# A two-layer conditioned-FFN kernel: first loads on three queues, B behind the mixture, and the end reordered

## The reference

```python
# layer 0
h = gelu(cond @ W0 + b0); h = gelu(h @ W1 + b1)
att = softmax(h @ W2 + b2)                          # 128 x 8
agg_w = einsum('bk,koi->boi', att, weight[..., 0]); agg_b = att @ bias_k
t = einsum('boi,bih->boh', agg_w, x) + agg_b[:, :, None]
gates = softmax of the two best of (t @ Wr.T) over 4 experts
x = x + sum_e gates_e * 16/sqrt(16) * (t @ A_e.T) @ B_e.T
# layer 1
o = grouped_conv1d(x, weight, 9 taps, 4 groups) + cond @ c_weight.T + fside
h = relu(layernorm(o @ gw1.T + gb1) * gamma + beta)
g = h @ gw2.T + gb2                                 # 8 experts, top 2, softmax over the two
counts = how often each expert is first, second, over all 4096 rows
w = gates of the experts whose count is at most the capacity
x = x + o @ weight.T + ((o @ lora_A_e) * w_e) @ lora_B_e / 16
```

## Time and profile before

| | us |
|---|---|
| runs of the kernel before, median of 3 | 305.37 (305.17 to 308.9) |
| the profiled execution's own time | 303.87 |
| its span (first to last recorded event) | 302.1 |
| TensorE busy | 290.3 (96%) |
| VectorE busy | 194.9 (64%) |
| ScalarE busy | 125.2 (41%) |
| GpSimd busy | 95.1 (31%) |

### The profile page before, as it was taken

One profiled execution on the slowest core, in us unless ns is written; L12 is line 12 of the kernel. 1 busy time (PEld: TensorE's weight loads), 2 busy tenths in 40 slices (PEclk: granted clock), 3 DMA queues, 4 the chain that ended last, 5 costly groups with the idle time before them and its releaser, 6 DMA issues.

```text
span 302.1 us, 6171 instructions
## 1 busy us (share of the span) xinstructions
PE 290.3 (96%) x1995; PEld 239.7 (79%) x1995; DVE 194.9 (64%) x503; ACT 125.2 (41%) x263; POOL 95.1 (31%) x124
## 2 busy tenths in 40 slices
PE   7999999999999999999999999999999999798994
PEld 6989967787888788879887978797868777586883
DVE  1445984734488448835793579366957645878785
ACT  3417743436523652356235622562256235111330
POOL 4342425132312331143114311431114116216650
PEclk9999999999999999999999999999999999999998
DMA  5696799992779289918892879386538860004887
GB/s 134 196 335 139 169 257 220 235 217 62 218 214 208 54 220 229 192 35 243 207 201 44 242 205 189 55 233 148 136 71 244 174 142 0 0 2 171 322 334 286
DMA packets 74255, 52.75 MB, mean 175 GB/s; under 512 B 44388, under 2 KB 61204, under 8 KB 74232
## 3 DMA queue, kind: packets, MB, share of 16 engines
q1 hardware_dynamic: 72792, 51.37, 67.3%
q10 hardware_dynamic: 1120, 1.07, 1.2%
q0 software_dynamic: 320, 0.02, 0.4%
HBM read 35.67 MB, written 16.78 MB: 174 GB/s over the span
## 4 chain that ended last, share of the span: by engine, by line
PE 65%; SPq 10%; DVE 10%; DMA 6%; issue 4%; ACT 2%; DVEq 0%; ACTq 0%
PE ps_g L1124 13%; PE ps_d L1124 12%; PE ps_c L1264 8%; PE ps_a L1085 6%; PE ps_t L1280 4%; SPq L352 4%; DMA xg<-x1d 3%; PE ps_a L1074 3%; DMA x1d<-xq 3%; PE ps_d L1305 3%; SPq L355 2%; PE ps_d L1306 2%; PE ps_v L1097 2%; PE ps_d L1491 1%; PE ps_d L1487 1%
## 5 line engine op out<-in xcount | busy, mean ns | idle before, releaser
L508 POOL TENSOR_TENSOR o1l<-o,o1h 128x512 fp32r<-128x512 f32 x30 | 39.3, 1311 | 149.3 <-ACT o L639 149.3
L1124 PE MATMUL ps_d<-wt_hi,o1h 128*128 128x336 f32 (+1 forms) x120 | 41.1, 342 | 0.3 <-DVE y_all L950 0.3
L1124 PE MATMUL ps_d<-wt_hi,o1l 128*128 128x336 f32 (+1 forms) x120 | 38.7, 323 | 0.0
L1124 PE MATMUL ps_d<-wt_lo,o1h 128*128 128x336 f32 (+1 forms) x120 | 38.6, 322 | 0.0
L1124 PE MATMUL ps_g<-wt_hi,o1h 128*128 128x336 f32 x112 | 35.7, 319 | 0.6 <-ACT tmp_all L654 0.4
L944 DVE TENSOR_TENSOR oT<-ps_c,biasT 128x512 f32<-128x512 f32 x32 | 21.9, 685 | 21.7 <-PE ps_c L1264 21.7
L1124 PE MATMUL ps_g<-wt_hi,o1l 128*128 128x336 f32 x112 | 35.5, 317 | 0.0
L1124 PE MATMUL ps_g<-wt_lo,o1h 128*128 128x336 f32 x112 | 35.4, 316 | 0.0
L1264 PE MATMUL ps_c<-xg,cw 96*32 96x512 f32 x256 | 34.1, 604 | 1.0 <-DMA xg<-x1d 1.0
L627 ACT ACTIVATE xq<-y_all 128x512 f32 (+1 forms) x29 | 31.8, 1150 | 7.0 <-DMA x1d<-xq 3.7
L1085 PEld LDWEIGHTS ps_a<-pm,xT 128*128 128x128 f32 x256 | 30.2, 192 | 1.4 <-issue 0.8
(11 more groups left out here) (249 smaller groups left out, 582.1 us busy)
## 6 DMA issues: line engine op xcount, KB each, us to landing
xg<-x1d SPq DMA_DIRECT2D x64, 254.0 KB, 4.8
xg<-x1d SPq DMA_DIRECT2D x32, 256.0 KB, 3.7
x1d<-xq SPq DMA_DIRECT2D x30, 256.0 KB, 3.4
xs<-in_x_dram SPq DMA_DIRECT2D x6, 1024.0 KB, 5.9
out_dram<-xT SPq DMA_DIRECT2D x16, 256.0 KB, 2.1
out_dram<-xg SPq DMA_DIRECT2D x16, 256.0 KB, 2.1
y_all<-in_x_dram ACTq DMA_DIRECT2D x2, 512.0 KB, 5.5
y_all<-in_x_dram SPq DMA_DIRECT2D x1, 1024.0 KB, 5.7
```

Of the source, the lines that this page charges most:

```text
L508: pool.tensor_tensor(lo, o1[t % 2][:, :, :], hi.bitcast(fp32), ALU.subtract).then_inc(s_o1l, 1)
L1124: last = T.matmul(bank[:, 0:columns], a[:, Q - 1 - q, :], w[:, q, first:first + columns], start=(q == 0 and n == 0), stop=(q == Q - 1 and ...
```

## The change

1. **First loads.** W2 is issued first on ScalarE's queue; b2 and the second half of x of step 0 go to SyncE's queue, behind W1; the context weights move behind the mixing bias; the four loads of B and the one of fside are issued by GpSimd, ahead of its copy of the mixing weights. SyncE's queue issues 13 loads ahead of the main weights' group where it issued 16, ScalarE's 4 where it issued 6.
2. **TensorE and VectorE at the start.** Three of the dummy product pairs between the attention's products go. The two small context products move from between the attention's products to behind x's transposes; B's transposes and their split move behind the mixture and its bias products.
3. **lora_B.** The high part is made in step 6 on ScalarE, before its last gate copy, the low part on GpSimd behind step 6's last split, into `gms` (now of type fp32r, with bitcasts where it was read as fp32) instead of `o1l`.
4. **Norm, counts, y.** In the last step `norm_last` runs between the one-hot comparison and the count sums of step 6. The counts come from one product over the four one-hot tiles at once (64 columns), and VectorE sums the five groups. y of tiles 1 and 2 is added before the counts are read, y of tile 3 after `lt_lo`.
5. **Last tile.** Its lora products, sum and store are done in two halves of 256 columns, the second in another PSUM bank (`ps_t`).

```diff
@@ SyncE, ScalarE, GpSimd: loads
-            sp.dma_start(ctxn, ctxw).then_inc(s_ld["ctx"], 16)
-            sp.dma_start(w2n, w2).then_inc(s_ld["w2"], 16)
+            sp.dma_start(b2b, b2.partition_broadcast(P)).then_inc(s_ld["b2"], 16)
+            sp.dma_start(xs_early[0][:, NT // 2:NT, :], x_v[0][:, NT // 2:NT, :]).then_inc(s_xh, 16)
...
-            for e in range(E0):
-                sp.dma_start(bn[:, :, e * R0:(e + 1) * R0],
-                             ffb[e].rearrange("(p c) r -> p c r", c=HC)).then_inc(s_ld["bn"], 16)
+            sp.dma_start(ctxn, ctxw).then_inc(s_ld["ctx"], 16)
...
+            for e in range(E0):
+                pool.dma_start(bn[:, :, e * R0:(e + 1) * R0],
+                               ffb[e].rearrange("(p c) r -> p c r", c=HC)).then_inc(s_ld["bn"], 16)
+            pool.dma_start(fsb, fside.partition_broadcast(P)).then_inc(s_ld["side"], 16)
             pool.wait_ge(s_ld["mixw"], 64)
...
+            act.dma_start(w2n, w2).then_inc(s_ld["w2"], 16)
...
-            act.dma_start(b2b, b2.partition_broadcast(P)).then_inc(s_ld["b2"], 16)
             act.dma_start(xs_early[0][:, 0:NT // 2, :], x_v[0][:, 0:NT // 2, :]).then_inc(s_xf, 16)
-            act.dma_start(fsb, fside.partition_broadcast(P)).then_inc(s_ld["side"], 16)
-            act.dma_start(xs_early[0][:, NT // 2:NT, :], x_v[0][:, NT // 2:NT, :]).then_inc(s_xh, 16)
@@ GpSimd and ScalarE: lora_B
-        lb_hi, lb_lo = b_hi, o1l[0][:, :, :].rearrange("p q m -> p (q m)")
+        lb_hi, lb_lo = b_hi, gms[:, :, :, :].rearrange("p t a c -> p (t a c)")
...
                 if at_step(s, NS - 1):
                     rstd(s)
+                if at_step(s, NS - 2):
                     pool.wait_ge(s_lbh, 1)
-                    pool.wait_ge(s_mp, s * NT + 1)
+                    pool.wait_ge(s_gtp, NS)
                     pool.tensor_tensor(lb_lo, lbn, lb_hi[:, :].bitcast(fp32), ALU.subtract).then_inc(s_lb, 1)
...
                 o_hi(s + 1, 0)
+                if at_step(s, NS - 2):
+                    act.wait_ge(s_ld["lora"], 16)
+                    nc.scalar.activation(lb_hi[:, :], lbn, ACT.Copy).then_inc(s_lbh, 1)
                 ga_out(3)
@@ VectorE: norm, counts, y
                     y_out(s, 0)
-                    choices_counted(s - 1)
-                    norm_last(s)
+                    choices_counted(s - 1, lambda: norm_last(s))
                     choices_weighted(s - 1)
...
+            y_out(NS - 1, 1)
+            y_out(NS - 1, 2)
             link, n = chain(dve, s_c3, 0)
             dve.wait_ge(s_cntp, 1)
-            link(V.tensor_scalar(allowed[:, :, :], ps_g[:, 0:2 * E1].rearrange("p (c e) -> p c e", c=2),
-                                 float(CAPACITY), None, ALU.is_le))
+            link(V.reduce_sum(cnt1[:, :, :], ps_g[:, 0:2 * E1 * (NT + 1)]
+                              .rearrange("p (t c e) -> p c e t", c=2, e=E1), AXX))
+            link(V.tensor_scalar(allowed[:, :, :], cnt1[:, :, :], float(CAPACITY), None, ALU.is_le))
...
-            y_out(NS - 1, 1)
-            y_out(NS - 1, 2)
-            y_out(NS - 1, 3)
             dve.wait_ge(s_lth, 1)
             V.tensor_tensor(lt_lo[0][:, :], ps_a[0][:, :], lt_hi[0][:, :].bitcast(fp32), ALU.subtract)\
              .then_inc(s_ltf, 1)
+            y_out(NS - 1, 3)
@@ TensorE: counts, last tile
             pe.wait_ge(s_cnt, 1)
-            for t in range(NT):
-                last = T.matmul(ps_g[:, 0:2 * E1], ones[:, :], oh[:, t, :, :].rearrange("p c e -> p (c e)"),
-                                start=False, stop=(t == NT - 1))
-            last.then_inc(s_cntp, 1)
+            T.matmul(ps_g[:, 0:2 * E1 * NT], ones[:, :], oh[:, :, :, :].rearrange("p t c e -> p (t c e)"),
+                     start=True, stop=True).then_inc(s_cntp, 1)
...
+                if at_step(s, NS - 1):
+                    for cols, bank in ((slice(0, H // 2), ps_l[NT - 1]), (slice(H // 2, H), ps_t)):
+                        high(NT - 1, cols, bank)
+                        low(NT - 1, cols, bank)
```

More of the change, by code:

```diff
@@ L422, in store @@
                 for t in range(NT):
-                    sp.wait_ge(s_yo[t], s + 1)
-                    sp.dma_start(out_v[bass.ds(s * NT + t, 1)].rearrange("n p h -> p (n h)"), yo[par][t])\
-                      .then_inc(s_out[par][t], 16)
+                    parts = 2 if at_step(s, NS - 1) and t == NT - 1 else 1
+                    n = H // parts
+                    for i in range(parts):
+                        sp.wait_ge(s_yo[t], s + i + 1)
+                        sp.dma_start(out_v[bass.ds(s * NT + t, 1)].rearrange("n p h -> p (n h)")[:, i * n:i * n + n],
+                                     yo[par][t][:, i * n:i * n + n]).then_inc(s_out[par][t], 16)
             steps(sp, store, 0, NS - 1)
@@ L903, in choices_counted @@
                     link(chosen)
+                    if between is not None:
+                        between()
                     link(V.reduce_sum(cnt1[:, :, :], oh[:, :, :, :].rearrange("p t c e -> p c e t"), AXX))
@@ L1059, in finish @@
                     for t in range(NT):
[L1060 removed]
                         wait(dve, s_out[par][t], k * 16)
[L1062 to L1063 removed]
+                        parts = 2 if at_step(s, NS - 1) and t == NT - 1 else 1
+                        n = H // parts
+                        for i in range(parts):
+                            dve.wait_ge(s_lp, s * NT + t + i + 1)
+                            V.tensor_tensor(yo[par][t][:, i * n:i * n + n], (ps_l[t], ps_t)[i][:, i * n:i * n + n],
+                                            y_all[:, bass.ds(s * ST + t * H + i * n, n)],
+                                            ALU.add).then_inc(s_yo[t], 1)
             steps(dve, finish, 0, NS - 1)
@@ L1185, in _ @@
             t1(0, xs_early[0], 3)
+            pe.wait_ge(s_ld["ctx"], 16)
+            T.transpose(ps_g[:, 0:C], ctxn, ident[0:C, 0:C]).then_inc(s_sp["ctxT"], 1)
             pe.wait_ge(s_ss["pm"], 1)
             u_products(0, (0,))
-            pe.wait_ge(s_bn, 1)
-            for c in range(HC):
-                last = T.transpose(ps_t[:, c * P:(c + 1) * P], bn2[:, c, :, :].rearrange("p d e -> p (d e)"), idp)
-            last.then_inc(s_sp["b"], 1)
+            pe.wait_ge(s_ss["ctxT"], 1)
+            T.matmul(ps_g[:, 0:C], condT, ctxT, start=True, stop=True).then_inc(s_sp["ctx"], 1)
             u_products(0, (1,))
@@ L1206, in _ @@
             last.then_inc(s_mbps, 1)
+            pe.wait_ge(s_bn, 1)
+            for c in range(HC):
+                last = T.transpose(ps_t[:, c * P:(c + 1) * P], bn2[:, c, :, :].rearrange("p d e -> p (d e)"), idp)
+            last.then_inc(s_sp["b"], 1)
             u_products(0, (2, 3))
```

72 lines of the change are left out of this document (32 added, 40 removed).

## The result

The changed kernel takes 311.65 us, the median of 4 executions (310.93 to 312.44), against 305.46 of the kernel before: 1.018 times the time by the means (1.020 by the medians), 95% interval 1.010 to 1.025. By the medians it is slower by 6.2 us, outside the range; that it is slower is clear, that it is so by more than 2% is not.

What follows compares the result with a forecast made beforehand. TensorE, busy 290.3 of 302.1 us, was taken as the bound, so only its gaps and both ends could pay: 0.9 start + 3.0 end + 0.1 last tile = 4.0, from 305.37 to 301.4 us; range 299.3 to 304.2.

Steps and rivals of the forecast that it cites:

- I count the exchange as nothing: Start, TensorE: two small context products, 0.2 us each, replace a dummy pair behind x's first transposes; net cost nothing.
- the 0.9 us that the start was to gain: Start: 0.65 us from x's earlier transposes plus 0.28 of spare time at VectorE's gate chain; bounds -0.2 and 1.7.
- B on GpSimd's queue: Start: B's four loads take 5.1 us to issue, land by 14.5, wanted at about 16.5, 1.5 us of cover.
- B comes late and the kernel is slower: Rival, start: slow GpSimd issues make TensorE wait for B, 6.6 us lost, 308.0 us; chance 0.06.
- x's first transposition: Start, TensorE: begins at 8.2 instead of 8.87, gain 0.65 us; between 7.4 and 9.1 depending on x's halves.
- SyncE's queue and the gate chain: Start: first DRAM write 2.0 us earlier removes the 0.60 wait; VectorE's gate chain then limits TensorE to 0.28.
- the start gives nothing: Rival, start: x's two halves share the DMA engines, so no gain there; 302.3 us, chance 0.17.
- The end: Last step, norm through low part: TensorE goes on at 270.9 instead of 273.89, gain 3.0 us; bounds 1.8 and 3.5.
- GpSimd's weighting: End: weighting of step 1 finishes at 269.1, TensorE waits some 0.3 us for it, inside the 3.0.
- lora_B's two operations: High part on ScalarE, low part on GpSimd, both ahead of copies that waited (2.98 and 3.98 us): free there.
- The last tile: Sum and store in halves: gain 0.1 us, bounds -0.6 and 0.4.
- The way from profile to median: Profiled execution lies 1.5 us under the 305.37 median; no other difference expected, so the gain is subtracted from the median.

Runs made afterwards that it cites:

- e2: Kernel before with only the dummy pairs the change removes taken out (four, at three places): 303.56, 303.65, 311.74, 311.5 us.
- e9: Kernel before with all six dummy pairs out between its first conditions product and x's third transposition: 306.78, 303.95, 311.94, 312.4 us.
- e1: Changed kernel with the removed dummy pairs put back: 309.43, 301.26, 312.02, 309.36 us.
- e7: Changed kernel with A and the router loaded ahead of x's second half and the dummy pairs back: median 301.98 us, 2 of 10 over 307.
- e5: Kernel before with only the end parts of the change, last tile not halved: 304.02, 300.12, 301.1, 305.09 us, ratio 0.987.
- e13: Changed kernel with the dummy pairs back and B's loads on SyncE's queue behind the context's weight: median 302.38 us, 0 of 12 over 307.
- e10: Changed kernel with the dummy pairs back and B's loads on SyncE's queue, ahead of the context's weight: 301.61, 310.58, 310.74, 301.64 us.
- e8: Changed kernel with its loads kept, the dummy pairs back and six more dummy products in TensorE's waits: median 303.15 us, 0 of 10 over 307.
- e3: Kernel before with only the end parts of the change, halved last tile included: 301.16 us, ratio 0.989, 0 of 10 over 307.
- e16: Kernel before with the end parts, last tile whole, and four dummy products ahead of the first convolution: 300.58 us, ratio 0.987.
- e4: Kernel before with only the start parts of the change: 314.21 us; three executions at 313.9 to 315.6, one at 304.91.

## Why the prediction was wrong

**The step that failed.** "The two small context products that now follow are in exchange for a dummy pair that stood there ... I count the exchange as nothing", and with it the three pairs taken out, which I booked under work saved. I had weighed dummies by what they occupy. Their work is the clock: e2 and e9 show 8 us in half of the executions for their removal alone. The second half of the step is the load of B, booked as free as long as nobody waits for it: with the dummies back, 3 of 4 executions still lay over 307 (e1), with A early besides 2 of 10 (e7). In the place of the 0.9 us that the start was to gain, the trace shows 10.3 lost at the first convolution.

The profile of before had a part of the evidence. This is TensorE's group of dummies there from 5 to 30 us (busy, mean ns, idle before):

```profile
L1145 PE MATMUL ps_d<-ones 128*128 128x128 f32 x14 | 4.1, 403 | 0.0
```

4.1 us of work that gives nothing, in a stretch where TensorE "has almost no gap". And the lengths of the earlier trace rows show that the clock wasn't at 1.00 all along, as I had read it: it came up only at some 10 us, 2 us ahead of the first products of 68 columns. I took the row of eight transpositions at 1.67 as their price; at full clock it is 1.10. The Trainium skill (TensorE: Matmul & The Clock Gate, HAM oscillation — how this bites in real kernels) says that waits for DMAs between a kernel's products throttle the clock again; I had not asked what the change did by that rule. The runs agree in kind: a fall behind the wait of 1.00 in e1, of 1.25 in e5 and of 1.79 in e9; e13 has a wait of 1.06 and no fall.

What stays open is why one execution of a kernel gets the clock in time and the next does not, and whether the long row keeps the clock down by its narrow products or by its moment.

**B on GpSimd's queue.** Forecast: issues of 1.3 per load, in time for its user with 1.5 to spare. The issues took 3.21 for four, 0.80 each, well under my 5.1, and no instruction of TensorE waited for B. The rival "B comes late and the kernel is slower" was nearest in the number (308.0), but its mechanism isn't there. But I asked only who waits for B, not who shares its engines. The rule that I cited from the Trainium skill (DMA: Bandwidth & Descriptors, Issuing engines are not separate DMA queues) I applied to x's halves alone. Its other victim was A, 1.0 to 1.3 late, which put a wait on TensorE where nothing covered it (e10: 0.20 with B behind it).

**x's first transposition.** Forecast 8.2; it came at 7.92, and at 8.0 to 9.3 in the runs with the changed start. The landing took 5.7 instead of 5.2 (6.6 in e7 and e8, 7.1 in e13). In most runs that lies between the two ends that I gave, 5.2 and 6.9, in e13 beyond. That it is the other half of x which delays it was not tested by itself; B's loads, too, were in flight in most of them. In e13 the transposition came at 9.32, with the wait of 1.06, and no gain was left.

**SyncE's queue and the gate chain.** In the changed kernel the slow clock hides both. Where the clock held, in e13, the first convolution came at 39.74 with a wait of 0.35 for the gather. The start's gain of 0.9 was not there: 0.0, though the clock came up earlier than before (7.78 against 10.15 in the two records). The rival "the start gives nothing" (302.3) was right about that, and wrong by 9 us all the same.

**The end.** Forecast 3.0, found 3.1 in the trace; the wait for the normed rows 0.46 of some 0.5; the sum over the counts 0.23 of 0.27; the low part came in time without y's sums ahead of it; GpSimd's weighting left a wait of 0.17 where I said 0.3. lora_B's two operations were free, and the running count takes 0.18 at most (once 1.07 in the earlier trace rows). Here forecast and mechanism agree. By the times e3 and e16 gained 3.7 and 4.3 on medians, about 1 more than the trace; they have fewer executions in the group just above than the kernel before, which may be that 1 us and wasn't tested.

**The last tile.** Forecast +0.1 with -0.6 as the lower end; the trace has -0.3, the medians -1.0. Wrong in sign: I let the last sum's end and a shorter transfer decide; the sum's end didn't move, and what lies behind it took 0.3 longer.

**The way from profile to median.** "I see no reason for another difference" of the 1.5 between the profiled execution and the median: the profile shows one execution out of groups at 303 to 305 and, rarely, at 307 to 310, and what the change did was to move its weight to the far group. No single trace of before could say how near that was, but one execution at 308.9 among the three of its runs could have asked the question; the later runs of it record mean clocks of 0.982 to 1.00. The range, built of terms of work and waits, had no term for a clock that falls. (It is also not what its bounds add up to, 299.8 to 304.4, but 299.3 to 304.2; 311.65 lies outside both.)

## What to carry to other kernels

Before taking dummy products out of a stretch, ask what the granted clock does without them, and test it by taking only them out, in several executions. Judge a moved load by everything in flight beside it, above all by the small load whose user has no cover, and follow it to a wait on TensorE: with waits of 1 us ahead of a long row of small products, many executions here were 8 us longer. Where executions fall into groups, give the share of each group, and compare on one chip; a median of four says little. And read the clock from the lengths of equal instructions before believing its column.

## What the runs showed of the hardware that was not expected

- TensorE stayed at 1.2 GHz while it was fully occupied: 5.00 of 5.00 us from 15 to 20 and from 20 to 25 in e4, granted clock 0.50, in products of 64 and 68 columns. With the clock up, the same products kept it up (e13: 1.00 from 10 to 35, 5.00 and 4.58 of 5 us busy from 15 to 25). In e8 it rose among transpositions of 128 columns (0.50 from 10 to 12, 0.92 from 12 to 14), and in before as well (at some 10 us); the runs don't separate the width from the moment.
- The same code has both courses: e4 took 304.91 once and 313.9 to 315.6 three times. What decides between them within an execution wasn't tested and stays open.
- The granted clock reads 1.00 ahead of the first change on record: until 34.19 in the changed kernel's profile and until 10.15 in that of before, beside lengths that are doubled. The lengths decide.
- A load of 512 short runs cost GpSimd 0.80 to issue, against 0.66 on SyncE's queue (2.63 for four in the earlier trace rows): 0.14 more, while the two points of the earlier trace rows had made me expect 1.3.
- Halving a store behind a halved sum: five issues at 2.74 against four at 2.43, and 0.3 us later at the end.
